# The next body's first k projection behind the second scores, and half of the quantization behind the first state chain, in the first group of a retention and FP4 linear kernel

## What is computed

```python
q = heads((x @ Wq + bq) * scaling)          # 16 heads of 64
k = heads(x @ Wk + bk)
v = heads(x @ Wv + bv)
D = where(causal, exp(decay * (i - j)), 0)
ret = einsum('bhid,bhjd->bhij', q, k) * D
ret = ret / clip(abs(ret.sum(-1)), 1.0)
g = groupnorm_per_head(einsum('bhij,bhjd->bhid', ret, v)) * gn_w + gn_b
attn = silu(x @ Wg + bg) * g @ Wo + bo

xq, xs = quantize_nvfp4(x, x_tensor_scale)   # amax of 16, e4m3 scale, e2m1 values
wq, ws = quantize_nvfp4(weight)
ffn = (xq * xs) @ (wq * ws).T * output_scale + bias
out = x0 + attn(xn) + ffn(xn)                # xn = layernorm(x0)
```

## Time and profile before

| what | value |
|---|---|
| timed runs | 2136.59, 2141.93, 2142.75 us; median 2141.93 |
| profiled execution | 2142.48 us; span from first to last instruction 2140.7 us |
| mean granted TensorE clock | 0.991 |
| TensorE busy | 2080.3 us, 97% of the span |
| VectorE busy | 1541.7 us, 72% |
| ScalarE, GpSimd busy | 685.9 us, 640.0 us |
| DMA | 275.61 MB, 129 GB/s over the span |
| first group (bodies 0 to 3) | from about 30 to about 269 us |

### The profile page before, as it was taken

How to read it: one execution, slowest core, us unless ns; L and a number is a source line. 1 busy time by engine, 2 the same in 40 slices (tenths; PEclk the granted TensorE clock), 3 DMA queues, 4 the chain that set the end, 5 groups by cost and what they waited for, 6 DMA issues and landing times.

```text
span 2140.7 us, 51098 instructions
## 1 busy us (share of the span) xinstructions
PE 2080.3 (97%) x18098; PEld 1053.5 (49%) x18098; DVE 1541.7 (72%) x4375; ACT 685.9 (32%) x1318; POOL 640.0 (30%) x456
## 2 busy tenths in 40 slices
PE   5988899999999999999999999999999999999999
PEld 3444444455455454555555555454555454555444
DVE  7899898988889877566767556767656767656732
ACT  5756623332223233322323322323322322322300
POOL 1323232332233333223332223233223233223220
PEclk8999999999999999999999999999999999999999
DMA  8878634334343443323333323333323333223343
GB/s 317 282 253 265 218 98 138 108 109 136 100 127 108 137 128 94 102 83 109 124 103 93 103 84 109 122 103 94 103 85 107 122 103 95 103 86 106 122 153 117
DMA packets 181686, 275.61 MB, mean 129 GB/s; under 512 B 117344, under 2 KB 117472, under 8 KB 181344
## 3 DMA queue, kind: packets, MB, share of 16 engines
q1 hardware_dynamic: 181600, 274.48, 39.8%
HBM read 204.18 MB, written 40.89 MB: 114 GB/s over the span
## 4 chain that ended last, share of the span: by engine, by line
PE 86%; DVE 11%; DMA 2%; issue 1%; ACT 0%; SPq 0%; DVEq 0%; ACTq 0%
PE mm L1288 54%; PE mm L1223 10%; PE tp L1223 6%; PE mm L1232 4%; PE tp L1298 3%; PE four L1338 3%; PE four L1351 2%; PE tp L1326 1%; PE four L1311 1%; PE four L1232 1%; PE tp L1251 1%; DVE wo L929 1%; DMA res<-in_w_f 1%; DMA parts<-wo 1%; DVE state L1041 1%
## 5 line engine op out<-in xcount | busy, mean ns | idle before, releaser
L1288 PE MATMUL mm<-xnT,wring 128*128 128x512 f16 x6144 | 1365.8, 381 | 13.8 <-DVE wring L929 6.8
L1288 PEld LDWEIGHTS mm<-xnT,wring 128*128 128x128 f16 x6144 | 598.2, 98 | 710.3 <-issue 25.2
L695 ACT ACTIVATE work<-four,gs 128x64 f32<-128x64 f32 x512 | 158.1, 414 | 554.2 <-DVE gs L1068 554.2
L556 POOL TENSOR_TENSOR yT<-gn,gate 128x512 f32 (+1 forms) x64 | 84.2, 1315 | 800.6 <-ACT gn L706 800.6
L1223 PE MATMUL mm<-wo,yT 128*128 128x512 f16 x960 | 214.1, 380 | 0.1
L1055 DVE BATCH_NORM_STATS2 gst<-four 128x6 f32<-128x64 f32 x512 | 73.5, 216 | 195.0 <-PE four L1351 194.8
L539 POOL TENSOR_TENSOR qparts<-qT,qparts 128x512 f16<-128x512 f32 x64 | 77.0, 1203 | 363.2 <-ACT qT L664 363.1
L539 POOL TENSOR_TENSOR kparts<-kT,kparts 128x512 f16<-128x512 f32 x64 | 84.2, 1316 | 225.1 <-ACT kT L664 225.1
L1223 PEld LDWEIGHTS mm<-wo,yT 128*128 (+1 forms) x960 | 91.0, 98 | 108.3 <-issue 0.2
L1223 PE MATMUL tp<-wo,yT 128*128 128x512 f16 x576 | 128.2, 379 | 0.0
L662 ACT ACTIVATE qparts<-mm,consts,down 128x512 f16<-128x512 f32 x64 | 49.7, 776 | 213.2 <-PE mm L1288 213.2
(11 more groups left out here) (198 smaller groups left out, 2648.8 us busy)
## 6 DMA issues: line engine op xcount, KB each, us to landing
wring<-parts SPq DMA_DIRECT2D x252, 512.0 KB, 3.9
xt<-in_x SPq DMA_DIRECT2D x34, 512.0 KB, 3.6
out<-res SPq DMA_DIRECT2D x32, 512.0 KB, 3.0
parts<-wo SPq DMA_DIRECT2D x28, 512.0 KB, 5.6
res<-in_x SPq DMA_DIRECT2D x28, 512.0 KB, 3.5
ftile<-in_w_f SPq DMA_DIRECT2D x12, 512.0 KB, 4.4
parts<-wring SPq DMA_DIRECT2D x8, 512.0 KB, 6.8
probs<-in_x SPq DMA_DIRECT2D x5, 512.0 KB, 4.6
```

The costliest lines, as they stand in the source:

```text
L556: nc.gpsimd.tensor_tensor(hi, gn[:], gate[:, u], ALU.mult)
L695: last = nc.scalar.activation(work[:, c * P + h * HD:c * P + (h + 1) * HD], ao[h][:, c * VW:c * VW + HD], ACT.Identity, bias=gs[:, 1, g:g ...
L1288: last = MM(mm[n % 2][:], wring[:, n, wj, k, :], xnT[:, parity, xj, k, :], start=(j == 0), stop=(j == 3 * KT - 1))
```

## The change

Two groups of instructions get another place, both in phase FIRST. On TensorE, bodies 0, 1 and 2 issue the next body's `project(0, 0)` behind `scores(1)`, ahead of `state_increments(1)`; bodies 1, 2 and 3 no longer issue it at their start. Its waits are those of the next body. On VectorE, bodies 1, 2 and 3 run quantization half 1 behind `states(0)`, no longer ahead of `mask_scores(0)`. ScalarE's, GpSimd's and SyncE's lists stay as they are.

```diff
@@ -1096,8 +1096,6 @@
                     quantize_scales(xt, x_ts, x_r6)
                     w("xq_moved", 0)
                     quantize_half(xt, 0)
-                    if i:
-                        quantize_half(xt, 1)
                     mask_scores(0)
                     if i == 0:
                         quantize_half(xt, 1)
@@ -1105,6 +1103,8 @@
                         in_scales(weight_scales)
                     scale_batch()
                     states(0)
+                    if i:
+                        quantize_half(xt, 1)
                     split_lo(i + 1, range(0, 2))
                     find_f_max(F_TILES[i][0])
                     group_norm(0)
@@ -1274,10 +1274,11 @@
                     finish_half(w, parity, q, 1, "t0", 1)
                     return
 
-                def project(u, n):
-
+                def project(u, n, ahead=0):
+
+                    w = waiter(pe, phase, i + ahead)
                     use = mm_use(u, n)
-                    if (phase, i, u) == (FIRST, 0, 0):
+                    if (phase, i + ahead, u) == (FIRST, 0, 0):
                         pe.wait_ge(lo_done, n + 1)
                     else:
                         w("w_" + MATS[n], u)
@@ -1354,7 +1355,8 @@
 
                 pe.wait_ge(s["xnT_ready"], 2 * CH)
                 pe.wait_ge(s["x_moved"], group * (CH * 2 * 16) + 16)
-                project(0, 0)
+                if phase != FIRST or i == 0:
+                    project(0, 0)
                 if phase == FIRST and i == 0:
                     pe.wait_ge(sums_read, 1)
                     sum_slices(0, 4, 4)
@@ -1388,6 +1390,8 @@
                 project(1, 3)
                 scores(1)
                 if phase == FIRST:
+                    if i + 1 < CH:
+                        project(0, 0, ahead=1)
                     state_increments(1)
                     attend_within(1)
                     transpose_g(0)
```

## The result

The changed kernel takes 2165.24 us (median of four runs, 2164.42 to 2167.8), the kernel before 2142.19 (four runs). The ratio is 1.0116 with a 95% interval of 1.0097 to 1.0134, and the medians differ by 23.1 us. (The ratios here are estimated from all the runs; they need not be the quotient of the two medians, which is 1.0108 in this case.) The profiled execution took 2165.0 us, its span is 2163.2. In the changed file the lines of TensorE's part stand one lower than before (L1289 a projection, L1312 scores, L1327 state increments, L1339 attention within, L1352 attention to earlier ones); VectorE's and SyncE's are the same, up to L1095.

What follows compares the result with a forecast made beforehand. VectorE's in-order list was taken to bound the first group, TensorE the rest. Weights 16.8, queue 4.0, VectorE's gain -3.3 and clock 5.5 made 23.0 us, added to 2141.93 for 2165 us; range 2149 to 2180.

Steps and rivals of the forecast that it cites:

- The upper end of the range: 37 us of added time, described as full clock price and a queue a little over its middle, giving 2179 us.
- What bounds the kernel: VectorE's in-order list sets the first group, so each microsecond there moves the end by as much; TensorE sets the rest.
- The rival on which TensorE is the bound here: First group: filling TensorE's waits counts, 13.6 us in all, so 2128 us; chance 0.04.
- Part 1, the weights: Bodies 0 to 2: the moved projection waits for its weight slice and delays VectorE's second state chains, +16.8 us.
- The rival of no measurable change: The weight slices are there when the second scores end; 2.6 us more, so 2145 us; chance 0.05.
- Part 2, the half and the queue: Bodies 1 to 3: the moved quantization half is free, but SyncE's queue delays a store: +4.0 us.
- The queue: SyncE, bodies 1 and 2: the split slice's store meets busy DMA engines, 2.0 us each, +4.0 us (0 to 12).
- The warning of no slack: First state chains: with the half moved, anything making TensorE late ahead of them becomes VectorE's wait; no size given.
- Part 3, VectorE's gain: Body 3: VectorE's waits of 2.46 us for attention and 0.88 us for ScalarE go, -3.3 us (-2 to -6).
- Part 4, the clock: TensorE: new gaps lower its clock, five at 1.1 us each, +5.5 us (bounds 0 and 14.5).
- Full price for every gap, the rival: TensorE's gaps each cost the full slow clock, 14.5 us, total 32.0, so 2174 us; chance 0.16.

Runs made afterwards that it cites:

- e1_proj_only: The changed kernel with the quantization half back in its old place, so only the projection moves, against the kernel before: 2155.39 us, 1.0075.
- e2_quant_only: The kernel before with only the second quantization half moved behind the first state chain: 2133.27 us, 0.9978; run again, 2134.64 us, 0.9978.
- e3_early_slice: The changed kernel with the k slice of the projection ahead loaded early from an already stored slot: 2142.20 us, 1.0021 against the kernel before.
- e7_late_move: The changed kernel with SyncE's transposition and next x load behind the k load in bodies 1 to 3: 2160.68 us, 1.0099 against the kernel before.
- e4_warm: The changed kernel with TensorE's gaps filled by matmuls whose results are not used: 2158.70 us, 1.0092 against the kernel before; again 2159.84 us, 1.0097.
- e8_quant_early_f: e2_quant_only with SyncE's raw tile load ahead of two slice loads and the last store: 2132.76 us, 0.9974 against the kernel before.
- e9_early_and_behind: e3_early_slice with the projection ahead also placed behind the second state increments: 2149.19 us, 1.0048 against the kernel before.
- e5_changed_again: The changed kernel run again, unaltered, beside the kernel before: 2165.57 us, 1.0126.

## Why the prediction was right

Forecast 2165 us (range 2149 to 2180), measured 2165.24. Not all of that agreement is merit: several terms were off, in both directions, and the starting point had luck in it. The 23.0 us were added to 2141.93, a median of three executions. Over 13 to 19 executions the kernel before took 2138.0 to 2138.7, while the changed kernel came to 2165.57 again, so its cost is nearer 27 us. Counted in the profiles from the first state chain of body 0, it is 24.7. The upper end of the range was also described wrongly: 37 us with the full clock needs 9 us for the queue, three quarters of its 12 and not a little over the middle.

**What bounds the kernel.** Right. VectorE's new waits in the first group reach the end of the program in full: 17.7 us of them in `e1_proj_only` for 17 us of time. The rival on which TensorE is the bound here falls with the same run: TensorE's waits ahead of its second increments were filled, and the kernel lost what VectorE waited more. `e2_quant_only` agrees. TensorE's waits of 2.8 to 3.1 us ahead of the first increments went, those ahead of the second rose by 1.9 to 2.1 (from 1.31 to 3.37 us in body 1), 2.9 us less in all, and the three bodies became 6.4 us shorter.

**Part 1, the weights.** Right in mechanism and size. The gap in body 0 was forecast at 2.3 us and is 3.11, the second chain at 93.4 and is at 93.36. That match has two errors in it. This execution was 1.6 us ahead at the first state chain of body 0 (72.36, before 73.92), where nothing had been changed yet, because its first projections ran at a higher clock; and the projection took 7.04 us, not 5.34. Counted from the first chain the body costs 7.7 us. For bodies 1 and 2, with their shares of queue and clock, 9.0 and 10.0 were forecast and 9.2 and 10.4 measured. `e3_early_slice` shows the cause by itself. The rival of no measurable change, slices that are there in time, had about the right price (2.6 us more than before; measured 4.0) and the wrong premise.

**Part 2, the half and the queue.** That the half is free as such was too careful: it gains, through the collision with GpSimd that it leaves. The queue: 4.0 forecast, 4.9 measured with `e7_late_move`. The transposition stands straight ahead of the store and delays the k load by 1.7 and 1.8 us, as told; but of the 4.9 us the traces show only 1.6 at the state chains that were to pay for it, so that the totals agree is in part luck. The warning of no slack was right: 0.86, 0.89 and 0.99 us of waits ahead of the first chains, 2.7 in all, which no term of the sum carried by that name.

**Part 3, VectorE's gain.** -3.3 forecast. `e2_quant_only` gives -4.9, and -4.0 the second time, with body 3 alone 3.6 us shorter and the others 2.1 and 0.7. In the changed kernel body 3 gains 2.6, with 1.0 us of a new wait in it.

**Part 4, the clock.** The term that was worked out wrongly. I counted five gaps and took 1.1 us for each, from a gap of half the length. There are six, since body 0's gap of 3.11 us counts as well, and their projections are 1.7 to 2.1 us longer, 11.7 in all. VectorE pays for the three that stand ahead of the second chains, 5.6 us, and for those at a body's opening only what comes through at the first chain, 2.7 us: 8.3. Taking the clock away in five of the six gives 4 to 7 us. So the size (5.5) came out, in part by luck, because a price too low per gap stood against cover that I hadn't counted. Full price for every gap, the rival, would have given 2174 us. (The Trainium skill, TensorE: Matmul & The Clock Gate, section on why this matters for your kernels, is borne out as to the gaps in the changed kernel: each of the six put the clock down, to 0.50 to 0.53 in the 2 us behind it, though the gap of 3.02 us in `e4_warm` did not. What it costs is a matter of who waits.)

**Where the combination comes from.** By medians the halves alone sum to 12.3 us and the whole is 23 to 28. The profiles, one execution each, show where the rest arises. Take a body's length from one second state chain to the next. With both halves body 1 is 6.8 us longer than the two halves alone make it, and body 2 4.9. Held against `e1_proj_only`, the first store comes 1.7 and 1.2 us later in these bodies (the lost slack is part of this), the way from it to the k load is 1.7 and 1.9 us longer (the queue), the load lands 0.5 and 1.0 us sooner, and the projection takes 1.8 and 2.1 us longer (the clock). These are 4.7 and 4.2 us. The other 2.1 and 0.7 are what the moved half gains when it is alone: in front of a chain that waits for the weights to land, VectorE's saved time only makes the wait longer. The forecast had no term for this. Body 3 adds 1.5 us and body 0 0.4, 13.5 in all.

**What stays open.** Where the remainder of the queue's 4.9 us lies, and whether the projection pays further back, past the attention, which wasn't tried; there it stands where it stood before.

## What to carry to other kernels

Before moving work into an engine's idle time, ask when its operands land and who is queued behind it: here a gap of 1.5 us was to take a projection of 5.3 us whose weights came 3 to 6 us after TensorE was ready for them, and even with the weights there it cost 9 us in one place and 15 in the next, since each stands ahead of another of VectorE's inputs. Read the bound from the stage and not from the run: TensorE's share of the chain rose while its filled gap made the kernel slower. And time each half of a change that has two, since here one was worth 4 to 5 us and the other hid it, and since the gain of the one vanished behind the wait of the other. When instructions of a fast engine get shorter, see whether its waits get longer by as much before calling it a gain.

## What the runs showed of the chip that I had not expected

- VectorE's instructions with two tensor inputs in SBUF stand still while GpSimd runs a tensor operation that began before them: in body 1 of `e8_quant_early_f` 0.16 us become 1.01, 1.04 and 1.08, each ending within 0.02 us of GpSimd's, and those with one input (L807, L793, L794: 0.15 us beside the same GpSimd instructions) don't. In the first group the layer norm grew by 5.5 us in this way, where earlier loads had freed 6.3. (The Trainium skill, SBUF — State Buffer, in its section on who interferes with whom, states it: a VectorE instruction with two SBUF inputs contends with a GpSimd instruction that reads SBUF, and the later one blocks until the first is through. The rows agree to within 0.02 us.)
- The price of a gap doesn't follow its length. Ahead of a projection of 5.34 us, 3.11 us of idle time cost 1.7, 5.4 to 5.9 us cost 1.8 to 2.1, and in `e7_late_move` 4.04 and 4.14 us cost 2.7 and 2.9. In `e9_early_and_behind`, where the short state increments stand between gap and projection, 3.39 and 3.37 us cost 1.1 and 2.2, and 1.48 nothing. In `e4_warm` 3.02 us cost nothing, in `e5_changed_again` 2.18 us cost 1.7. The same 2.41 us near the start, at 46 us, cost 1.7 us in the profile before and nothing in the one after.
- A 512 KB store issued 1.9 us behind a transposing DMA and a 512 KB load landed after 5.1 us, alone after 3.4.
